# Down projection of a fused attention and FFN block: plain products, and one-level Strassen products over five K ranges

## The reference, cut to what matters

```python
def reference(x, ctx, gate_codes, gate_scales, up_codes, up_scales, down_codes, down_scales):
    x = x + xattn(layernorm(x), ctx, ctx)          # 16 batches of 128 x 1024
    Wg = dequant_nf4(gate_codes, gate_scales)      # (2752, 1024)
    Wu = dequant_nf4(up_codes, up_scales)          # (2752, 1024)
    Wd = dequant_nf4(down_codes, down_scales)      # (1024, 2752)
    h = layernorm(x)                               # 2048 rows of 1024
    inter = silu(h @ Wg.T) * (h @ Wu.T)            # 2048 x 2752
    return x + inter @ Wd.T                        # 2048 x 1024, all float32
```

## Time and profile before

| | us |
|---|---|
| median of three executions | 1600.88 |
| profiled execution, span | 1597.2 |
| TensorE busy in it | 1558.9 |
| DVE busy | 1051.3 |
| ACT busy | 807.6 |
| POOL busy | 73.1 |
| mean granted TensorE clock | 0.994 of full |

### The profile page before, as it was taken

One profiled execution on the slowest core, in us unless ns is written; L12 is line 12 of the kernel. 1 busy time (PEld: TensorE's weight loads), 2 busy tenths in 40 slices (PEclk: granted clock), 3 DMA queues, 4 the chain that ended last, 5 costly groups with the idle time before them and its releaser, 6 DMA issues.

```text
span 1597.2 us, 20530 instructions
## 1 busy us (share of the span) xinstructions
PE 1558.9 (98%) x7296; PEld 1296.5 (81%) x7296; DVE 1051.3 (66%) x1118; ACT 807.6 (51%) x869; POOL 73.1 (5%) x107
## 2 busy tenths in 40 slices
PE   3999999999999999999999999999999999999999
PEld 3888888888888888888888888888778888888887
DVE  2999878888888888888888888875422224422221
ACT  3688756666566666556556566645311114211110
POOL 1444200000000000000000000000000000000000
PEclk8999999999999999999999999999999999999999
DMA  4444233323333333323323333326564433433440
GB/s 158 153 164 158 107 109 119 130 102 114 108 114 109 107 108 113 103 96 118 111 101 112 108 114 111 105 96 227 196 248 148 148 114 133 148 128 119 148 146 28
DMA packets 94429, 202.73 MB, mean 127 GB/s; under 512 B 5571, under 2 KB 50627, under 8 KB 90563
## 3 DMA queue, kind: packets, MB, share of 16 engines
q1 hardware_dynamic: 94402, 202.40, 36.8%
HBM read 150.99 MB, written 51.38 MB: 127 GB/s over the span
## 4 chain that ended last, share of the span: by engine, by line
PE 89%; DVE 4%; DMA 3%; issue 1%; SPq 1%; ACT 1%; DVEq 1%; POOL 0%; ACTq 0%; POOLq 0%
PE bank L1000 20%; PE bank L1001 20%; PE bank L999 20%; PE bank L1052 8%; PE bank L1053 8%; PE bank L1054 8%; DMA F<-in_x 2%; PE bank L950 1%; DVE bn L751 1%; PE bank L977 1%; DMA F<-inter_scratch 1%; DVE F L781 1%; DVE R L809 1%; DVEq L754 1%; SPq L389 1%
## 5 line engine op out<-in xcount | busy, mean ns | idle before, releaser
L540 ACT ACTIVATE F<-F 128x1024 f32<-128x1024 bf16 x504 | 491.2, 1048 | 130.5 <-DVE F L718 124.0
L999 PE MATMUL bank<-R 128*128 128x512 f32 x1376 | 535.5, 389 | 0.0
L1001 PE MATMUL bank<-R 128*128 128x512 f32 x1376 | 535.3, 389 | 0.0
L1000 PE MATMUL bank<-R 128*128 128x512 f32 x1376 | 535.3, 389 | 0.0
L999 PEld LDWEIGHTS bank<-R 128*128 128x128 f32 x1376 | 258.3, 188 | 53.9 <-DVE R L741 0.2
L1000 PEld LDWEIGHTS bank<-R 128*128 128x128 f32 x1376 | 258.3, 188 | 53.6
L1001 PEld LDWEIGHTS bank<-R 128*128 128x128 f32 x1376 | 258.3, 188 | 53.5
L663 ACT CAST R<-F 128x2816 fp32r<-128x2816 f32 x30 | 76.8, 2559 | 347.4 <-PE bank L1058 321.7
L1052 PE MATMUL bank<-R 128*128 128x512 f32 x642 | 250.0, 389 | 2.5 <-DVE R L898 2.5
L1053 PE MATMUL bank<-R 128*128 128x512 f32 x642 | 249.8, 389 | 0.0
L1054 PE MATMUL bank<-R 128*128 128x512 f32 x642 | 249.7, 389 | 0.0
(11 more groups left out here) (83 smaller groups left out, 1135.0 us busy)
## 6 DMA issues: line engine op xcount, KB each, us to landing
F<-inter_scratch SPq DMA_DIRECT2D x30, 1408.0 KB, 7.3
inter_scratch<-F SPq DMA_DIRECT2D x84, 256.0 KB, 13.7
F<-in_gu_codes SPq DMA_DIRECT2D x41, 512.0 KB, 13.2
F<-in_gu_scales SPq DMA_DIRECT2D x41, 512.0 KB
F<-in_d_codes SPq DMA_DIRECT2D x22, 512.0 KB, 14.1
F<-in_d_scales SPq DMA_DIRECT2D x22, 512.0 KB
wd_scratch<-F SPq DMA_DIRECT2D x22, 512.0 KB, 13.4
F<-in_x SPq DMA_DIRECT2D x16, 512.0 KB, 3.5
```

The source lines that it names most:

```text
L540: nc.scalar.activation(lines[q % LR], code7[s], ACT.Copy, bias=offset, scale=slope).then_inc(line_ready, 1)
L999: pe.matmul(dst, hi, xh[:, tb, t, :], start=(t == 0), stop=False)
L1000: pe.matmul(dst, hi, xl[:, tb, t, :], start=False, stop=False)
L1001: i = pe.matmul(dst, lo, xh[:, tb, t, :], start=False, stop=(t == HT - 1))
```

## The change

The first 20 of 22 K tiles are handled in five ranges of four K tiles (`NR`), and the rows in eight pairs of tiles (`NM`). One step `g` of 40 (`NG`) takes one pair of row tiles and one range: a 2 x 2 block problem, whose blocks are 128 x 256 of `inter` and 256 x 512 of the weights. It is computed with Strassen's seven products in the form with fewer additions (Winograd's), where plain products need eight. A product (`product`) is six matmuls of 512 columns.

Each step needs, beside its 42 matmuls:

- SP: one load of 512 KB of `inter` (`load_stage`), two steps ahead.
- ACT: h of the three blocks used as they are (`hi_a`, 128 x 768), h of the four sums S1 to S4 (`hi_s`, 128 x 1024), and four copies of PSUM to SBUF (`snapshot`, 128 x 512): of the bank that sums several products after its first, third and fifth part, and of the third product.
- DVE: the sums S1 to S4 (`s_forms`, four operations of 128 x 256), l of the blocks (`lo_a`, 768) and of the sums (`lo_s`, 1024), and four additions of a PSUM bank to the output `yacc` in SBUF (`y11` and `late_sums`, 128 x 512).
- POOL: four additions of the copies to `yacc`, three of 128 x 512 and one of 128 x 1024.

Per range the weights are loaded as one block of 2 MB (`load_base`, at the third step of the range before), their sums T1 to T4 are made by DVE in steps 4 to 7 of the range before (`t_form`, 128 x 1024), and the seven weight forms are split at the border of the ranges: seven ACT copies of 128 x 1024 (`hi_w`), and seven subtractions of 128 x 1024 (`lo_w`), five on DVE and two on POOL (`POOL_SLOTS`). There is one set of the split forms, so each copy waits for the product of the last step that reads the old one.

The output of all rows, 2048 x 1024, lies in SBUF (`yacc`). It begins as x: eight loads of 1 MB (`load_y`), where half of the gate and up part's input lay. The last two K tiles (`rest`, five matmuls for each of four outputs of a pair) are plain products in the steps of the last range. Their weights are split in the sixth step of range 4. Each pair's output is stored in two DMAs of 512 KB in the last range (`store_pair`). No hardware loops are used in this part: all engines run straight code. The matmuls of the part are 40 x 42 + 8 x 20 = 1840, where before there were 32 x 65 = 2080.

```diff
+            def load_stage(g):
+                r, m = g // NM, g % NM
+                for q in range(2):
+                    sp.wait_ge(inter_stored[q], 32 * (4 * r + 4))
+                wait(sp, la_ready, g - 1)
+                sp.dma_start(stage[g % 2]..., inter_dram[2 * m:2 * m + 2, :, 4 * r:4 * r + 4, :]...).then_inc(stage_in[g % 2], 16)
...
+            load_stage(0)
+            load_stage(1)
...
+            load_base(0)
             store_block(c, 2)
             store_block(c, 3)
             store_block(FULL, 0, HALF)
             store_block(FULL, 1, HALF)
+            sp.wait_ge(gate_done, FULL * TB + 3)
+            for m in range(NM // 2):
+                load_y(m)
             store_block(FULL, 2, HALF)
+            sp.wait_ge(gate_done, FULL * TB + 4)
+            for m in range(NM // 2, NM):
+                load_y(m)
             store_block(FULL, 3, HALF)
...
+            for g in range(NG):          # SP
+                if g + 2 < NG:
+                    load_stage(g + 2)
+                if m == 2 and r + 1 < NR:
+                    load_base(r + 1)
...
+            for g in range(NG):          # POOL
+                if g:
+                    add_u4(g - 1)
+                if m == 0 and r:
+                    for i in POOL_SLOTS:     # (4, 6)
+                        lo_w(r, i)
...
+                pool.wait_ge(a_ready, g + 1)
+                add(yacc[:, m, 0, 0:WIDE], snap_a).then_inc(a_added, 1)
+                pool.wait_ge(q_ready, g + 1)
...
+                add(yacc[:, m, 1, :]..., snap_q.unsqueeze(1).to_broadcast([P, 2, WIDE])).then_inc(q_added, 1)
+                pool.wait_ge(u2_ready, g + 1)
+                pool.wait_ge(q_added, g + 1)
+                add(yacc[:, m, 1, 0:WIDE], snap_u2).then_inc(u2_added, 1)
...
+            for g in range(NG):          # ACT
+                turn = m == NM - 1 and r + 1 < NR
+                if r == NR - 1 and m + 1 < NM:
+                    hi_rest(m + 1)
+                snapshot(snap_a, x, 1, g, a_added, a_ready)
+                if turn:
+                    hi_w(r + 1, 0)
+                if g + 1 < NG:
+                    hi_a(g + 1)
+                if turn:
+                    hi_w(r + 1, 1)
+                snapshot(snap_q, bankQ, 3, g, q_added, q_ready)
+                snapshot(snap_u2, x, 4, g, u2_added, u2_ready)
+                if turn:
+                    for i in (2, 3, 4):
+                        hi_w(r + 1, i)
+                if g + 1 < NG:
+                    hi_s(g + 1)
+                snapshot(snap_u4, x, 6, g, u4_added, u4_ready)
+                if turn:
+                    for i in (5, 6):
+                        hi_w(r + 1, i)
+                if r == NR - 2 and m == 5:
+                    for k in range(2):
+                        nc.scalar.copy(restw[k][0], restw_in_f[k]).then_inc(hrw_ready, 1)
+                if r == NR - 2 and m == NM - 1:
+                    hi_rest(0)
...
+            def late_sums(g):            # DVE; gather waits for the product and for the POOL addition named
+                y = yacc[:, g % NM]
+                gather(y[:, 1, 0:WIDE], bankV, 7, g, u2_added, y21_done)
+                dve.wait_ge(u4_ready, g + 1)
+                gather(y[:, 1, WIDE:], bankX[g % 2], 6, g, q_added, y22_done)
+                gather(y[:, 0, WIDE:], bankY, 5, g, u4_added, y12_done)
...
+            for g in range(NG):          # DVE
+                if g:
+                    lo_s(g)
+                if m == 0 and r:
+                    lo_w(r, 3)
+                    lo_w(r, 5)
+                if g:
+                    late_sums(g - 1)
...
+                if turn:
+                    lo_w(r + 1, 0)
+                if g + 1 < NG:
+                    s_forms(g + 1)
+                    lo_a(g + 1)
+                if r == NR - 1 and m + 1 < NM:
+                    lo_rest(m + 1)
+                y11(g)
+                if r + 1 < NR and 3 <= m < 7:
+                    t_form(r + 1, m - 3)
+                if turn:
+                    lo_w(r + 1, 1)
+                    lo_w(r + 1, 2)
...
+                if r == NR - 2 and m == NM - 1:
+                    lo_rest(0)
+            late_sums(NG - 1)
...
+            for g in range(NG):          # PE
+                if not fresh:            # the last range
+                    pe.wait_ge(lrw_ready, 2)
+                    pe.wait_ge(lr_ready, m + 1)
...
+                    rest(bankZ, 1, 1, True).then_inc(z_done, 1)
+                    pe.wait_ge(y11_done, g)
+                    rest(bankW, 0, 0, False)
+                    pe.wait_ge(y21_done, g)
+                    rest(bankV, 1, 0, False)
+                    pe.wait_ge(y12_done, g)
+                    rest(bankY, 0, 1, False).then_inc(rest_done, 1)
+                pe.wait_ge(la_ready, g + 1)
...
+                product(g, 0, x, a11, True)
+                wait(pe, y11_done, g)
+                product(g, 1, bankW, a12, fresh)
+                pe.wait_ge(ls_ready, g + 1)
+                wait(pe, q_ready, g)
+                product(g, 2, bankQ, s3, True)
+                pe.wait_ge(a_ready, g + 1)
+                product(g, 3, x, s2, False, True)
+                wait(pe, y12_done, g)
+                product(g, 4, bankY, s4, fresh)
+                pe.wait_ge(u2_ready, g + 1)
+                product(g, 5, x, s1, False, True)
...
+                wait(pe, y21_done, g)
+                product(g, 6, bankV, a22, fresh)
```

## The result

| | before | after |
|---|---|---|
| median of the runs, us | 1599.95 (runs beside after) | 1630.47 (1627.76 to 1634.79) |
| ratio to before | 1 | 1.0193 [1.0175, 1.0211] |
| span of the profiled execution, us | 1597.2 | 1626.0 |
| matmuls in down | 2080 | 1840 |
| down, first to last matmul, us | 474.6 | 499.8 |

The forecast of 1593 was wrong in sign, and the time lies outside the range too. The count of matmuls fell as the change says, yet the part became 25 us longer: the matmuls alone take 1840 x 0.2267 = 417.1, and the other 82.7 us of the part are stalls and a low clock, where before had 3.1. A T step is one in which a T sum delays PE, and a step is "over" by what it takes beyond its 9.52 us.

The account below looks back on a forecast made before the run. TensorE bounds the kernel: down's time is matmul count times distance between starts. 1542.6 without stalls + 11.5 + 20 + 10.5 + 2.7 + 2 = 1589.3, with 3.7 to the median 1593 us; 8 in 10 range 1570 to 1618.

Parts of the forecast that it names:

- PE's part and the tail: Down: 1840 matmuls at 0.2267 us take 417.1 us, two tile borders go; 6.3 us follow the last matmul.
- The start: Before step 1's sixth product: 8.4 MB of output loads hold back the third block load, 11.5 us with slow clock.
- The costs without exclusion: Down's stalls from queue orders alone, DVE and POOL not hindering each other: 1.5 us a border, 7.5 the last.
- the weights of the last K tiles: Step 6 of range 4: two extra ACT copies and two DVE subtractions make lo_s late, 2.7 us.
- second rival: Down steps: the meeting of DVE and POOL costs little, 27 us of stalls, 1573 us in all; chance 0.22.
- If they exclude each other, but for 0.14 each: 10.0 - 1.4 = 8.6 us of 9.52: Every down step: DVE's two-SBUF-input operations and POOL's additions run almost one at a time, leaving 0.9 us a step.
- The first rival: Down steps: POOL and DVE exclude each other whole, 9.4 us a step, 1617 us in all; chance 0.30.
- A T sum (+1.08) is absorbed by the 1.3 us in hand: Steps with a T sum: lo_a's 1.3 us lead over the next step's first product covers the added 1.08 us.
- Borders: 6.7 each and 2 for the clock forecast: First three range borders: 9.8 us added, less 1.3 in hand and 1.8 spare, 20 in all; 2 for slow clock.
- the clock behind all stalls after the start: PE in down: lowered clock after the border stalls, put at 2 us in all.
- the last border: Fourth range border: late splits and additions delay rest products, 7.5 us, plus 3 for waits on POOL's l: 10.5.
- The third rival: All of down: straight code and late waits feed PE worse, 28 us on top, 1621 us; chance 0.06.

Follow-up runs that it names:

- number 4: The changed kernel with six of the eight loads of x into the output spread over range 1, one a step: 1621.38 us, 1.0124 of before.
- number 2: The changed kernel with POOL's additions cut to one column, each behind memsets that keep POOL's time but read nothing: 1573.62 us, 0.9833 of before.
- Number 3: The kernel before, with 200 idle POOL additions of 128 x 512 beside its down part: 1631.65 us in a single run, where before had 1599.93.
- Number 6: The changed kernel without the T sums of ranges 2 to 5, waits and the 2 MB load kept: 1606.63 us, 1.0034 of before.
- numbers 1 to 3: The first of these: the changed kernel with POOL's additions on one column, waits and order kept, 1577.28 us; the others are number 2 and Number 3.
- Number 10: The changed kernel with q added from PSUM, loads spread, last weights split earlier, all weight subtractions on DVE, late sums earlier at the last border: 1577.05 us.

## Why the prediction was wrong

**PE's part and the tail** held. 1840 matmuls at 0.2267 between starts; the tail was 5.9 us for 6.3. Down began at 1120.4 for 1119.2, and the median lies 4.5 above the span for 3.7: 1.6 us together with the tail's 0.4 less.

**The start** held: 9.3 us for 11.5, at the named place, by the named load (number 4 took it away whole).

**The costs without exclusion** held as well. 1.5 us for a border measured 1.9, 7.5 for the last one 9.5, 2.7 for the weights of the last K tiles 4.0, the whole second rival 1573 for 1573.6 (number 2). So the orders of the four queues were followed through rightly, though each of these costs came out 0.4 to 2 us too low, low clock included. One bound was worked out wrongly and had no effect on the sum: 1408 KB in 7.3 us are some 195 GB/s and not 180.

**The failed step is "If they exclude each other, but for 0.14 each: 10.0 - 1.4 = 8.6 us of 9.52", and what followed from it.** I saw the rule on POOL's side in one collision, had no row for DVE's, and took the middle "between nothing and whole operations". Number 3 measured DVE's side: held for 1.08 of the 1.28 us of one POOL addition. So 0.20 an operation runs beside the other, not 0.14, but for POOL's four operations and not for all ten: a step uses 10.0 - 4 x 0.20 = 9.2 us (an estimate from that row), and has 0.3 to spare instead of 0.9. The first rival's 9.4 was nearer. Two conclusions hung on the 0.9:

- *"A T sum (+1.08) is absorbed by the 1.3 us in hand": 0 forecast, 27.5 us measured, the largest error.* The 1.3 us was lo_a's slack with the engines apart, and I spent it after I had already filled the step with exclusion. In the trace a T sum is not 1.08 us more but 2.06: it waits for a POOL addition, and lo_s behind it meets the next one (2.30). One addition more in the queue lets DVE meet one POOL operation more. Number 6 takes 21.5 us of it away. 1.7 of the 27.5 are low clock, in step 22.
- *Borders: 6.7 each and 2 for the clock forecast, 22 in all; 9.25 each measured, 27.8 in all.* I subtracted 1.3 us in hand and 1.8 spare from the 9.8 added. Of the 27.8, 6.4 are low clock, so the stalls are 21.4 for 20, or 7.1 each. That is near the 6.7, but partly by luck of where it is counted: another 1.4 to 1.6 us of PE's delay before each border step stand in the T row of the table. With both, a border stalls for 8.7 us, and 9.8 less twice the 0.3 spare would have been 9.2.

**A second term was too small: 2 us for the clock behind all stalls after the start.** The rows at a granted clock of 0.50 give 6.4 us at the three borders, 1.7 in step 22, 1.7 in step 30 and 1.9 in step 32, 11.7 in all. The prediction priced one such stretch, behind the start, at 1.7 us, and took 2 for all the rest, where six came, 1.5 to 2.6 us each.

The weights of the last K tiles (6.1 for 2.7, 1.7 of it clock) and the last border (11.7 for 10.5, 1.9 of it clock) are off by little more than this. Terms together, clock in its place: 27.5 + 5.8 + 3.4 + 1.2 - 2.2 = 35.7; with the clock apart, T sums 25.8, borders 1.4, weights 1.7, last border -0.7, clock 9.7, start -2.2, which is the same. And with 1.6 for the beginning, the tail and the median 37.3; 1630.5 - 1593 is 37.5.

**The first rival** had the mechanism, and its borders (10), last border (13) and start were right to a few us. It ended at 1617 because it priced a T sum at 1.0 beyond the 1.3 in hand, 2.7 us a range, where 6.9 were measured on average, and took 3 us for the clock. It was given 0.30; the rows held one collision for it and none against it, and that "no row shows DVE waiting" was the absence of a case, not a sign. What the Trainium skill states in "SBUF — State Buffer", "Who interferes with whom", is borne out on both sides by numbers 1 to 3: DVE's two-input operations and POOL's reading ones hold each other up, and a PSUM input or a memset takes no part.

**The third rival** (straight code and waits) fell: steps 0, 2, 3, 9 to 11, 17 to 19 and 25 to 27 take 9.52 us to the hundredth.

**Left open.** What decides who comes next: with both queues full the two engines mostly take turns, operation by operation (five DVE forms in 12.25 us beside three or four POOL operations), but in number 3 one POOL addition stood through two DVE operations, and the runs don't tell why. Number 10 still has borders of 7 us. A kernel with no POOL addition at all was not tried: taken from PSUM, the three that are left would bring DVE's step to 6.6 + 1.2 + 3 x 0.69 = 9.9 us, over PE's 9.52 (an estimate from the durations shown), so it is not plain that this would gain.

## What to carry to other kernels

Before work is given to POOL beside a busy DVE, add the two engines' times for the operations that read SBUF (DVE's with two SBUF inputs) as if they were one engine, and ask whether that sum fits the step: here it was 10.0 of 9.52 us, and each engine alone looked free. An operation with one PSUM input is outside this sum, so an addition to an output belongs on the engine that can take it straight from its bank. And slack that was found with the engines apart may be spent once: in a step that is already full by a shared resource it is gone.

## What the runs showed of the hardware

- A held operation shows in the trace as a longer one, and not as idle time. DVE looks 80 to 90% busy in the slices and is at work for some 70%: the waits must be read off the mean duration by form (1739 for 1222 ns), and no view of waits names the releaser.
- One POOL addition of 512 columns (1.28 us) holds a DVE operation for up to 1.1 us; one long DVE operation is held by one addition, not by several (2688 columns: 4.05 us at most, 2.96 in before). A POOL addition can be held by two DVE operations in a row (5.75 us, beside twice 2.14).
- POOL's memset (0.312 us for 256 columns) does not hold DVE, with 600 of them in the down part.
- The clock: in the 7.59 us that PE stood idle before p5 of step 1 it fell to the 1.2 GHz level, and the first matmul behind it took 0.79 us, as did the one behind a border's 3.81 us; behind the T step's 1.79 us of idle time the first took 0.50. Yet in step 22, behind 1.78 us of idle time, the clock was at the lower level 1.1 us later, with PE at work. The low clock cost 1.5 to 2.6 us a border, half of the time in which PE worked at it. The windows (last columns: granted clock, DMA share, GB/s): one within the start stall, with the queue full and no matmul, where 0.62 is a mix of both levels; one at the first border; one in step 22:

```profile
1140.00:1143.00 3.00, 0.00 (x0) 0.00 (x0) 0.40 (x2) 0.40 (x1) 0.00 (x0) 0.62 1.00 377
...
1219.30:1226.00 6.70, 5.20 (x12) 3.64 (x12) 6.70 (x4) 0.59 (x1) 6.70 (x3) 0.50 0.00 0
...
1383.10:1386.40 3.30, 3.30 (x10) 2.53 (x9) 3.27 (x5) 0.59 (x1) 1.76 (x1) 0.50 0.00 0
```
